# A hybrid block on one core: the expert bias as a constant feature, and sums of weighed values in the maxima's bank

## The chip, the cores and the metric

One core of a Trainium2 chip runs the kernel. The metric is the device time of one execution in microseconds. The kernel before was run three times.

## The reference

The block has four residual parts, over 4 sequences of 512 tokens with 128 features:

```python
x = x + attn_a(layernorm(x))   # 16 heads of 8, rope, causal softmax
x = x + ffn(layernorm(x))      # 8 experts, top 2 of a sigmoid gate, and one shared expert
x = x + attn_b(layernorm(x))   # short convolution, a scan over time, a gate
x = x + ffn(layernorm(x))      # the same weights again

# in ffn, H = 512, exact gelu:
h  = gelu(einsum('td,ehd->teh', xf, W1) + b1)
eo = einsum('teh,edh->ted', h, W2) + b2
combined = einsum('ted,te->td', eo, weights)
shared = gelu(xf @ Ws1.T + bs1) @ Ws2.T + bs2
```

`layernorm` has no scale and no shift, so the 128 features of a normed token sum to zero.

## The kernel before

**Attention** (about 26 to 225 us). The work goes by pairs of heads, 8 pairs for each sequence, 32 in all, numbered n. For pair n TensorE (PE) makes raw scores in three S units, of which VectorE (DVE) takes row maxima (`row_max`) and splits each into two bf16 numbers (`split_max`, L1883). PE turns them (`turn_max`, L1325), ScalarE (ACT) copies them out of PSUM (`copy_max`), and the SP queue places them by DMA as two more rows of the transposed queries (`place_max`, L623). Then PE makes transposed scores less the maximum in three T units (`scores_T`, L1340), ACT takes their exp (`exps`), and PE weighs the values with them (`weigh_values`). S runs two pairs ahead of T. After every second pair ACT copies the weighed values to SBUF (`take_weighed`, L960), PE turns and sums them with four fp32 products (`weighed_T`, L1375), and DVE divides by the sum of the exps (`divide`, L1891 and L1892).

PSUM has eight banks. Banks 0 to 5 are three slots of two, which the units of `ring_order` take in turn: S, T, the projections of the next sequence, the output projection, and the sums "w". A unit may start once the unit three places before it has been read. Bank 6 holds the weighed values, bank 7 (`Q2_BANK`) the turned maxima, each pair in one half of it.

Beside it the expert weights are loaded by ACT's queue (`ffn_loads`, L1020), and their largest magnitude is found on DVE in 16 pieces (`find_tops`). From pair 17 on ACT and DVE split the scaled weights into two f16 parts. GpSimd (POOL) does rope for the sequences 1 to 3 (`rope`, L768 and after), adds the output bias (`add_bias`), and reduces the bounds of the scales over partitions.

**Experts.** Each of the two ffn parts picks experts (`gates`, `choose`, `ranks`, `place`), and POOL scatters each token row, as two f16 parts scaled by `X_SCALE`, to its experts' lists in DRAM (L875). `map_tiles` (DVE) finds the expert of each of NT = 39 tiles of 128 rows. The tile stages (`tiles`, about 297 to 375 and 507 to 587 us) are a loop over k on PE: turn tile k (L1600), up products of tile k - 1, down products of tile k - 3 (L1626, L1627). Up is a bias product over 96 rows (L1606), then 12 products of 128 columns (L1612): high by high, low by high, high by low for each quarter of the 512 hidden features. ACT makes the gelu of tile k - 1 (L1155) and its high half (L1160), DVE the row's destination (L2123), the copy of the turned tile (L2129), the low half (L2135) and the sum of the down results (L2143). SP loads weights and rows, POOL scatters the results (L884). Tile s can have its gelu only once the low half of tile s - 3 is made, for three buffers.

The bias product multiplies `bias_rows` (each expert's bias in three bf16 parts, made on POOL by `bias_table`) by `which` (one column for each tile that picks the expert, made in `map_tiles`, L2098).

PE's order of work is written out by hand; each engine runs its own list in order, with waits on semaphores.

## Time and profile before

| | us |
|---|---|
| three runs | 608.64, 609.64, 613.06 |
| median | 609.64 |
| profiled execution | 606.08 |
| its span | 604.2 |

| engine | busy us | share of the span |
|---|---|---|
| PE, matmul | 501.5 | 83% |
| PE, weight load | 320.3 | 53% |
| DVE | 432.9 | 72% |
| ACT | 331.9 | 55% |
| POOL | 265.1 | 44% |

The mean granted clock of TensorE is 0.942 of full speed. A matmul's record is longer than the time until the next may start, since matmuls overlap: periods are read from starts. A wait is written with the engine and the line that ended it; where that engine had long been done, something else did. A releaser "remote" or "another core or an unknown queue" is one that the profile doesn't know.

### The profile page before, as it was taken

How to read it: one execution, taken by the hardware profiler on the slowest of the kernel's cores; microseconds unless marked ns; L12 is line 12 of the kernel's file. 1: busy time of each engine (PE TensorE's matmuls, PEld its weight loads, DVE VectorE, ACT ScalarE, POOL GpSimd, SP SyncE). 2: the span in 40 equal slices, each digit the busy share in tenths (PEclk: the TensorE clock that was granted, in tenths of full speed). 3: DMA queues.
4: the chain of work that ended last, by engine and by line, in shares of the span. 5: the costliest groups of instructions: out<-in, count | busy, mean ns of one | idle time of the engine just before them, and what ended most of it. 6: DMA issues, size and time to landing. Idle time of an engine off the chain costs nothing.

```text
span 604.2 us, 14288 instructions
## 1 busy us (share of the span) xinstructions
PE 501.5 (83%) x5019; PEld 320.3 (53%) x5021; DVE 432.9 (72%) x1162; ACT 331.9 (55%) x509; POOL 265.1 (44%) x247
## 2 busy tenths in 40 slices
PE   7778879878888888679999987879989977989950
PEld 2335556545656545334688775224545544878730
DVE  5658897686787968566377874798789663767745
ACT  1337556654777652546377863246657833757730
POOL 5509550045000037777046555373256770555550
PEclk9999999996999988888999999869999998999985
DMA  4863533441421370111588651997000016777516
GB/s 119 221 254 108 143 108 90 113 120 47 129 60 55 109 240 1 40 50 45 154 233 235 200 179 41 258 195 110 10 28 28 31 50 179 220 215 208 168 42 208
DMA packets 85708, 76.14 MB, mean 126 GB/s; under 512 B 9645, under 2 KB 72614, under 8 KB 85382
## 3 DMA queue, kind: packets, MB, share of 16 engines
q1 hardware_dynamic: 76320, 57.86, 36.6%
q0 software_dynamic: 4544, 9.38, 4.5%
q10 hardware_dynamic: 4774, 7.98, 3.7%
q8 instruction: 42, 0.69, 0.5%
q14 instruction: 28, 0.23, 0.1%
HBM read 37.88 MB, written 30.88 MB: 114 GB/s over the span
## 4 chain that ended last, share of the span: by engine, by line
PE 27%; DVE 9%; issue 5%; ACT 5%; another core or an unknown queue 4%; DMA 3%; POOL 1%; SPq 1%; ACTq 0%; DVEq 0%; POOLq 0%
PE ps L1612 6%; PE ps L1626 4%; PE ps L1627 3%; PE ps L1483 3%; DMA arena<-y_dram 2%; PE ps L1606 2%; DVE probs L2135 2%; ACT arena L1155 1%; PE ps L1560 1%; PE ps L1538 1%; DVE x_all L2164 1%; PE ps L1698 1%; DVE x_all L2160 1%; PE ps L1600 1%
## 5 line engine op out<-in xcount | busy, mean ns | idle before, releaser
L884 POOL DMA_INDIRECT y_dram<-arena,goes_to x78 | 85.0, 1090 | 90.5 <-DVE goes_to L2123 65.7
L1874 DVE TENSOR_REDUCE max_words<-ps 128x2 f32<-128x256 f32 (+3 forms) x128 | 98.0, 817 | 24.4 <-PE ps L1316 24.2
L955 ACT ACTIVATE probs<-ps 128x768 f32<-128x768 f32 (+1 forms) x96 | 81.1, 885 | 50.0 <-PE ps L1345 49.8
L730 POOL TENSOR_TENSOR rstd<-var_eps,minus_half 128x4 f32<-128x4 f32 x16 | 17.5, 1094 | 147.5 <-DVE var_eps L1841 147.5
L1155 ACT ACTIVATE arena<-ps,up_back 128x512 f32<-128x512 f32 x78 | 53.0, 680 | 52.1 <-PE ps L1612 28.6
L875 POOL DMA_INDIRECT rows_dram<-probs,idx x64 | 68.5, 1071 | 25.6 <-issue 18.6
L1626 PE MATMUL ps<-w,probs 128*128 x312 | 60.5, 273 | 11.7 <-DVE probs L2135 10.9
L1612 PE MATMUL ps<-arena 128*128 128x128 f16 x936 | 64.9, 219 | 4.0 <-DVE arena L2129 3.7
L2135 DVE SCALAR_TENSOR_TENSOR probs<-arena,hid_scale,probs 128x512 f16<-128x512 f32 x78 | 58.4, 748 | 11.5 <-ACT probs L1160 5.7
L1612 PEld LDWEIGHTS ps<-arena 128*128 128x128 f16 x936 | 57.8, 97 | 16.2 <-issue 8.7
L1483 PE MATMUL ps<-w,ident_f 128*128 128x512 f16 x184 | 56.3, 428 | 11.5 <-ACT arena L1111 3.3
L1160 ACT ACTIVATE probs<-arena,hid_scale 128x512 f16<-128x512 f32 x78 | 56.3, 722 | 2.6
L1627 PE MATMUL ps<-w,probs 128*128 x312 | 56.0, 219 | 0.6 <-issue 0.6
L2143 DVE TENSOR_REDUCE arena<-ps 128x128 f32<-128x256 f32 x78 | 32.9, 421 | 28.8 <-PE ps L1627 20.8
L1340 PE MATMUL ps<-heads_arena 64*128 64x512 bf16 (+3 forms) x256 | 38.2, 312 | 14.3 <-ACT probs L955 7.5
L1311 PE MATMUL ps<-heads_arena 62*128 62x128 bf16 (+3 forms) x256 | 36.5, 305 | 9.8 <-DVE max_words L1874 8.2
L1365 PE MATMUL ps<-probs,v_tok 128*32 128x256 f32 (+3 forms) x512 | 42.8, 452 | 2.0 <-ACT probs L955 2.0
L1626 PEld LDWEIGHTS ps<-w,probs 128*128 128x128 f16 x312 | 30.5, 98 | 18.6 <-issue 15.1
L1483 PEld LDWEIGHTS ps<-w,ident_f 128*128 128x128 f16 x184 | 18.0, 107 | 36.0 <-issue 13.7
L1316 PE MATMUL ps<-mask_qk,neg_eye 64*128 64x128 bf16 x512 | 34.3, 218 | 0.0
L1345 PE MATMUL ps<-mask_kq,neg_eye 64*128 64x128 bf16 x512 | 32.3, 221 | 0.0
L1627 PEld LDWEIGHTS ps<-w,probs 128*128 128x128 f16 x312 | 30.5, 98 | 1.1 <-issue 1.0
(242 smaller groups left out, 1033.7 us busy)
## 6 DMA issues: line engine op xcount, KB each, us to landing
arena<-weights_dram SPq DMA_DIRECT2D x78, 256.0 KB
rows_dram<-grids SPq DMA_DIRECT2D x64, 260.0 KB, 4.0
heads_arena<-q_words SPq DMA_DIRECT2D x45, 128.0 KB, 2.4
qk_sb<-rows_dram SPq DMA_DIRECT2D x78, 65.0 KB
arena<-in_w ACTq DMA_DIRECT2D x2, 2304.0 KB
weights_dram<-w SPq DMA_DIRECT2D x2, 1152.0 KB, 8.0
arena<-y_dram SPq DMA_DIRECT2D x16, 128.0 KB, 5.2
arena<-y_dram ACTq DMA_DIRECT2D x16, 128.0 KB, 5.3
```

Source lines behind the costliest of these rows:

```text
L875: nc.gpsimd.indirect_dma_start(rows_dram[r].ap(), bass.IndirectOffsetOnAxis(ap=idx[:, r, b, t, k:k + 1], axis=0), xrow_words_of(r, b)[:, t ...
L884: nc.gpsimd.indirect_dma_start(y_dram.ap(), bass.IndirectOffsetOnAxis(ap=goes_to[:, n % AT_GO:n % AT_GO + 1], axis=0), y_t[:, n % YT, :], ...
L955: nc.scalar.activation(probs[:, n % 2, :, PROB_AT[u]:PROB_AT[u] + size], ps[:, of:of + 2, 0:size], ACT.Exp).then_inc(slot_free[slot_of(("T ...
L1155: nc.scalar.activation(hid_t[:, n % HT, :], ps[:, of, :], ACT.Gelu, scale=up_back[:]).then_inc(bank_free[of], 1)
L1160: nc.scalar.activation(hid16_t[:, n % HT, 0, :], hid_t[:, n % HT, :], ACT.Identity, scale=hid_scale[:]).then_inc(high_t_ready, 1)
L1365: mm = pe.matmul(ps[group:group + OW, PV_BANK, j * P:L], v_flat[:, at_v:at_v + OW], probs[:, n % 2, h, at[j]:at[j] + L - P * j], start=(p ...
L1483: pe.matmul(ps[:, to, :], ident_f16[:], w1[:, 0, 0, :], start=True, stop=True, skip_group_check=True)
L1612: mm = pe.matmul(ps[:, to, c * P:(c + 1) * P], w1t[:, s % WT, w, c * P:(c + 1) * P], xgT[:, n % GT, v, :], start=False, stop=(v == 1), ski ...
L1626: pe.matmul(halves, hid16_t[:, n % HT, 0, c * P:(c + 1) * P], parts, start=(c == 0), stop=False, skip_group_check=True)
L1627: mm = pe.matmul(halves[:, 0, :], hid16_t[:, n % HT, 1, c * P:(c + 1) * P], parts[:, 0, :], start=False, stop=(c == C - 1), skip_group_che ...
L1874: ins = nc.vector.tensor_reduce(max_words[:, n % 2, :, t], ps[:, of:of + 2, o:o + keys], AX.X, ALU.max)
L2135: nc.vector.scalar_tensor_tensor(hid16_t[:, n % HT, 1, :], hid_t[:, n % HT, :], hid_scale[:], hid16_t[:, n % HT, 0, :], ALU.mult, ALU.subt ...
```

## The change

Two things are changed.

**The bias as a feature.** Since a normed token's features sum to zero, W1 x is also the sum over the first 127 features of (w_d - w_127) x_d. Feature 127 is then free: it carries the constant 1 (times `X_SCALE`, in the high part, and 0 in the low part), and row 127 of the experts' weights carries the bias. The host puts b1 into row 127 of `w1`, and gives `last_w1`, the row w_127 of all experts repeated for 128 partitions, 4096 fp32 values each. ACT's queue loads it into the room of the split weights, and POOL subtracts it from the raw weights after the first rope, in two instructions. `find_tops` takes the pieces of W2 first, and those of W1 after the subtraction. The bias product, its tables and their waits go, and the first up product of each quarter starts the accumulation. The shared expert keeps its bias in ACT's gelu.

**The sums in bank 7.** The maxima of all pairs now lie in the first quarter of the bank, and the sums of weighed values its upper half. The unit "w" leaves the ring. `weighed_T` stands before the third T unit, not after it, and waits for the copy of the next maximum and for the division before it; `turn_max` waits for the last division; ACT copies the weighed values before the first exp. The order in which banks are given after attention is changed too.

```diff
-        if n >= 2 and n % 2 == 0:
-            order += [("w", n // 2 - 1)]
-RINGS = {"all": (7, 1, 3, 5, 6, 2, 4, 0), "y": (0, 1), "wide": (2, 3, 4), "rest": (5, 6, 7)}
+RINGS = {"all": (1, 3, 5, 7, 6, 0, 2, 4), "y": (0, 1), "wide": (2, 3, 4), "rest": (5, 6, 7)}
...
+        def max_columns(n):
+            return ps[0:4 * TT, Q2_BANK, (n % 2) * (P // 2):(n % 2 + 1) * (P // 2)].bitcast(BF16)
+
+        def sums_at(start, end):
+            return ps[:, Q2_BANK, L // 2 + start:L // 2 + end]
...
@@ pool
             rope(1)
+            pool.wait_ge(ffn_in, 16 * len(ffn_loads))
+            pool.wait_ge(last_w1_loaded, 16)
+            for half in range(2):
+                of = slice(half * E * F // 2, (half + 1) * E * F // 2)
+                raw = arena[0:D - 1, of]
+                nc.gpsimd.tensor_tensor(raw, raw, last_w1[0:D - 1, of], ALU.subtract).then_inc(less_last, 1)
             add_bias(2)
             rope(2)
...
-            bias_table()
+            pool.wait_ge(pv_made, PAIRS)
+            set_constants(xrow)
@@ act
                 nc.scalar.dma_start(whole(dst), src).then_inc(ffn_in, 16)
+            nc.scalar.dma_start(last_w1, last_w1_in).then_inc(last_w1_loaded, 16)
...
-                exps(n, 0)
                 if n >= 2 and n % 2 == 0:
                     take_weighed(n // 2 - 1)
+                exps(n, 0)
                 exps(n, 1)
@@ pe, turn_max
                     pe.wait_ge(max_copied, n - 1)
+                if n >= 4:
+                    pe.wait_ge(sums_free, (n - 2) // 2)
@@ pe, weighed_T
-                to = give(("w", g))
+                if g >= 1:
+                    pe.wait_ge(sums_free, g)
+                pe.wait_ge(max_copied, min(2 * g + 4, PAIRS))
                 pe.wait_ge(weighed_ready, g + 1)
...
                 scores_T(n, 1)
-                scores_T(n, 2)
                 if n >= 2 and n % 2 == 0:
                     weighed_T(n // 2 - 1)
+                scores_T(n, 2)
@@ pe, tiles
-                pe.wait_ge(bias_ready, 1)
...
-                    pe.matmul(ps[:, to, :], bias_rows[0:BIAS_ROWS, :], which[0:BIAS_ROWS, s, :].unsqueeze(2).broadcast_to([BIAS_ROWS, C, P]),
-                              start=True, stop=False, skip_group_check=True)
...
@@ dve
+                if k == 0:
+                    dve.wait_ge(less_last, 1 if (piece + 1) * PIECE <= E * F // 2 else 2)
...
-                for c in range(C):
-                    nc.vector.tensor_scalar(which[:, :, c], expert_of[:], grids[:, MOD_AT + c:MOD_AT + c + 1], None, ALU.is_equal)
@@ host
-        "w1": w1.transpose(2, 0, 1),
+        "w1": np.concatenate([w1[:, :, 0:D - 1].transpose(2, 0, 1), np.concatenate([b1[0:E], w1[E:, :, D - 1]], 0)[None]], 0),
...
-        "b1e": np.tile(a["L0_ffn_b1"].reshape(E * C, P), (3, 1)),
+        "last_w1": np.repeat(w1[0:E, :, D - 1].reshape(1, E * F), P, 0),
```

## Rows read from the trace of the kernel before

**Rows 1.** Busy time by stretch: us, then each engine, clock, DMA share, GB/s.

```profile
core 0: us, PE busy (x) PEld busy (x) DVE busy (x) ACT busy (x) POOL busy (x), PEclk, DMA share, GB/s
40.00:80.00 40.00, 34.68 (x497) 21.45 (x499) 33.57 (x55) 25.07 (x40) 28.26 (x17) 1.00 0.38 109
302.00:374.00 72.00, 65.15 (x850) 54.98 (x847) 52.57 (x147) 49.88 (x74) 41.11 (x38) 1.00 0.63 185
510.00:585.00 75.00, 65.22 (x856) 55.34 (x853) 54.55 (x150) 51.87 (x76) 41.74 (x38) 1.00 0.61 182
```

**Rows 2.** Timeline of PE over one tile: start, length, work, idle before and releaser.

```profile
335.58 0.28 PE L1600 MATMUL ps<-ident_f,qk_sb 128*128 128x128 f16 x2
335.69 0.38 PE L1606 MATMUL ps<-weighed,bias_rows 96*128 96x512 bf16 x1
335.91 0.83 PE L1612 MATMUL ps<-arena 128*128 128x128 f16 x12
...
337.24 0.27 PE L1600 MATMUL ps<-ident_f,qk_sb 128*128 128x128 f16 x2
```

**Rows 3.** Timeline of PE and ACT, 329 to 334 us.

```profile
329.69 0.83 PE L1612 MATMUL ps<-arena 128*128 128x128 f16 x12
...
332.43 0.69 ACT L1155 ACTIVATE arena<-ps,up_back 128x512 f32<-128x512 f32 x1 [2.15 <-remote]
...
333.78 0.67 ACT L1155 ACTIVATE arena<-ps,up_back 128x512 f32<-128x512 f32 x1
```

**Rows 4.** Waits in the first tile stage, 300 to 375: total us, times, longest.

```profile
ACT arena L1155 <- remote: 8.4, 4, 2.2
...
PE ps L1626 <- DVE probs L2135: 5.6, 8, 1.5
```

**Rows 5.** Waits in the second tile stage, 510 to 585 us.

```profile
PE ps L1626 <- DVE probs L2135: 5.3, 8, 0.9
```

**Rows 6.** Timeline of DVE in the second map of tiles.

```profile
496.43 0.71 DVE L2098 TENSOR_SCALAR weighed<-weighed,grids 128x39 bf16<-128x39 f32 x4
```

**Rows 7.** Timelines of PE and of DVE in pair 22.

```profile
171.94 0.34 PE L1340 MATMUL ps<-heads_arena 64*128 64x384 bf16 x2
...
172.88 0.28 PE L1340 MATMUL ps<-heads_arena 64*128 64x256 bf16 x2 [0.49 <-ACT probs L955]
...
173.44 1.08 PE L1375 MATMUL ps<-fold,weighed 128*128 128x64 f32 x8
174.45 0.23 PE L1311 MATMUL ps<-heads_arena 62*128 62x128 bf16 x2
...
175.23 0.22 PE L1325 MATMUL ps<-ident,max_words 128*16 128x128 bf16 x1
...
173.49 0.17 DVE L1883 TENSOR_TENSOR max_words<-max_words 128x8 bf16<-128x8 f32 x1
174.55 0.26 DVE L1891 RECIPROCAL rec<-ps 128x16 f32<-128x16 f32 x1 [0.90 <-PE ps L1375]
174.84 0.29 DVE L1892 TENSOR_TENSOR att<-ps,rec 128x128 f32<-128x128 f32 x1
```

**Rows 8.** The start: SP's and PE's timelines, and the stretch of the loads.

```profile
30.81 13.97 SPq L623 DMA_DIRECT2D heads_arena<-max_rows  x6
...
40.27 0.39 PE L1340 MATMUL ps<-heads_arena 64*128 64x512 bf16 x2 [1.76 <-DMA heads_arena<-max_rows]
...
28.00:40.00 12.00, 8.64 (x63) 4.02 (x64) 7.16 (x11) 3.06 (x5) 2.04 (x2) 1.00 0.98 391
```

**Rows 9.** POOL's timeline at the second rope; all splits of maxima (min/median/max ns).

```profile
68.45 2.35 POOL L768 TENSOR_TENSOR rope_c<-q_words,k_words 128x1024 f32<-128x1024 f32 x1 [6.53 <-ACT q_words L991]
...
L1883 DVE TENSOR_TENSOR max_words<-max_words x32: 170/171/2040, 30.0 to 210.7; 128x8 bf16<-128x8 f32 x32
```

**Rows 10.** DVE and PE timelines at the bounds, and the stretch at half clock.

```profile
130.95 2.39 DVE L1932 SCALAR_TENSOR_TENSOR bounds<-bounds 128x1 f32<-128x1 f32 x1
...
136.97 0.61 PE L1311 MATMUL ps<-heads_arena 62*128 62x512 bf16 x2 [3.97 <-DVE max_words L1874]
...
135.10:145.30 10.20, 8.29 (x71) 5.26 (x73) 6.99 (x19) 1.81 (x3) 9.21 (x6) 0.50 0.06 16
```

More of the change, by code:

```diff
@@ L58 @@
 PIECE = X * F // PIECES
+TOPS_OF = [(k, piece) for k in (1, 0) for piece in range(PIECES)]
 PRODUCTS = [(0, 0), (1, 0), (0, 1)]
@@ L110, in ring_order @@
                 order += [(name, steps[n])]
-    return order + [("w", QUADS - 1), ("at", B - 1), ("wo", B - 1)]
+    return order + [("at", B - 1), ("wo", B - 1)]
 TURN = {unit: i for i, unit in enumerate(ring_order())}
@@ L383, in hybrid_block_kernel @@
         tile_row, weight_row, tile_expert = (weighed[:, NT * i:NT * (i + 1)].bitcast(I32) for i in range(4, 7))
-        which = part(weighed, 7 * NT, [NT, C], BF16)
         expert_of, tiles_past, first_row, list_end = (weighed[:, NT * i:NT * (i + 1)] for i in range(4))
@@ L831, in residual, with set_constants @@
                 nc.gpsimd.tensor_tensor(x_all[:, b], x_all[:, b], xsf[:, b], ALU.add).then_inc(residual_ready, 1)
[L833 to L849 removed]
+            def set_constants(rows):
+                nc.gpsimd.memset(rows[:, :, :, D - 1], X_SCALE)
+                link(nc.gpsimd.memset(rows[:, :, :, 2 * D - 1], 0.0))
             def split_rows(r, b):
@@ L858, in split_rows @@
                     pool.wait_ge(scattered[b - 2], 16 * 2 * TT * 2)
-                high, low = (xrow_of(r, b)[:, :, k * D:(k + 1) * D] for k in range(2))
-                link(nc.gpsimd.tensor_copy(high, xf_of(r, b)))
-                nc.gpsimd.tensor_tensor(low, xf_of(r, b), high, ALU.subtract).then_inc(rows_ready, 1)
+                if g == 0:
+                    set_constants(xrow4)
+                high, low = (xrow_of(r, b)[:, :, k * D:(k + 1) * D - 1] for k in range(2))
+                tokens = xf_of(r, b)[:, :, 0:D - 1]
+                link(nc.gpsimd.tensor_copy(high, tokens))
+                nc.gpsimd.tensor_tensor(low, tokens, high, ALU.subtract).then_inc(rows_ready, 1)
             def scatter(r, b):
@@ L977, in copy_max @@
                     act.wait_ge(max_placed[n % 2], 32 * (n // 2))
-                nc.scalar.copy(max_rows[:, n % 2, :], half_bank(n)[0:4 * TT, 0:P]).then_inc(max_copied, 1)
+                nc.scalar.copy(max_rows[:, n % 2, :], max_columns(n)).then_inc(max_copied, 1)
             def pre_queries(a):
@@ L1094, in last_rows_high @@
                 act.wait_ge(scattered[B - 3], 16 * 2 * TT * 2)
-                nc.scalar.copy(xrow_of(1, B - 1)[:, :, 0:D], xf_of(1, B - 1)).then_inc(last_high_ready, 1)
+                nc.scalar.copy(xrow_of(1, B - 1)[:, :, 0:D - 1], xf_of(1, B - 1)[:, :, 0:D - 1]).then_inc(last_high_ready, 1)
             def gates(r, b):
@@ L1886, in divide @@
                 a, q = divmod(g, 4)
-                of = take(("w", g))
+                dve.wait_ge(sums_full, g + 1)
                 if q == 0 and a >= 1:
                     dve.wait_ge(slot_full[slot_of(("at", a - 1))], filled(("at", a - 1)))
-                sums = ps[:, of, 0:TT * Q * VW].rearrange("p (t h w) -> p t h w", t=TT, h=Q)
+                sums = sums_at(0, TT * Q * VW).rearrange("p (t h w) -> p t h w", t=TT, h=Q)
                 core_link(nc.vector.reciprocal(rec[:], sums[:, :, :, HD]))
@@ L2050, in last_rows_low @@
                 dve.wait_ge(last_high_ready, 1)
-                high, low = (xrow_of(1, B - 1)[:, :, v * D:(v + 1) * D] for v in range(2))
-                nc.vector.tensor_tensor(low, xf_of(1, B - 1), high, ALU.subtract).then_inc(last_rows_ready, 1)
+                high, low = (xrow_of(1, B - 1)[:, :, v * D:(v + 1) * D - 1] for v in range(2))
+                nc.vector.tensor_tensor(low, xf_of(1, B - 1)[:, :, 0:D - 1], high, ALU.subtract).then_inc(last_rows_ready, 1)
             def place(r, b):
@@ L2332, in shape_constants @@
     grids[:, ONES_AT:ONES_AT + E] = 1.0
-    for c in range(C):
-        grids[:, MOD_AT + c] = np.where((rows < BIAS_ROWS) & (rows % C == c), rows // C % E, -1)
-    grids[:, PART_AT:PART_AT + 3] = rows[:, None] // (E * C) == np.arange(3)[None, :]
     grids[:, TOK_AT:TOK_AT + B * TT] = SPARE + 2 * (rows[:, None] + P * np.arange(B * TT))
```

62 lines of the change are left out of this document (20 added, 42 removed).

## Prediction, before the change was run

> **What bounds the kernel now.** I read the stretches first. In the two tile stages PE is busy 65 of 72 and 65 of 75 us at full clock, with ACT and DVE near 50 each [rows 1]: PE is the first suspect, with little room behind it. In attention (the row of 40 to 80 us stands for it) PE is busy 34.7 and DVE 33.6 of 40: no engine is full, two are nearly, so there the order of the units in the three-slot ring decides.
>
> Next the timeline of one tile. From the turn of one tile to that of the next, 335.58 to 337.24, PE needs 1.66 us without a gap, and the bias product stands 0.11 us behind the turn in the same queue. Its record says 0.38 us, but the first up product starts 0.22 us after it (512 columns at 2.4 GHz are 0.213): the 0.38 holds overlap, and 0.22 is what PE spends [rows 2].
>
> Then what else a tile needs. ACT's two passes repeat every 333.78 - 332.43 = 1.35 us when work is queued [rows 3]. That is below 1.66, and it stays below 1.44 = 1.66 - 0.22, by 0.09 only. And ACT is not always fed: the up products of one tile started at 329.69 and were through at 330.52, yet ACT's gelu, idle 2.15 us, began at 332.43, its releaser unknown to the profile [rows 3]. PE's results are thus sometimes seen some 2 us late, for a reason that I can't name. PE pays when its down product waits for the halves that DVE makes of that late gelu: 8 such waits, 5.6 us, in the first tile stage, 8 waits, 5.3 us, in the second [rows 4, 5].
>
> **Part 1: no bias product.** One for each of 39 tiles in two stages, 78 products go, 78 x 0.22 = 17.2 us of PE. Not all comes back. Between the up products of a tile and its down product lie two periods of PE's loop, so the slack that hides the chain gelu, high, low shrinks by 2 x 0.22 = 0.44 us. Each of the 8 waits of a stage grows by that: 8 x 0.44 = 3.5. A stage of 39 tiles gives 39 x 0.22 - 3.5 = 5.1 us, two give **10.2 us**. Ends: 17.2 if no wait grows; 4 if ACT, with only 0.09 us per tile to catch up, never recovers from one late signal before the next. I take the middle since only 8 of 39 tiles show the wait.
>
> POOL's table of ten small steps and the wait on it go too. Nothing in the waits names it as a releaser: 0. Of the map of tiles, four instructions on DVE go, 0.71 us in one row with overlap, 0.6 in its place [rows 6]. In the second stage PE and SP wait for the map: **-0.6 us**; in the first it lies beside shared products: 0. DVE, ACT and POOL now split 127 of 128 columns, and POOL sets a few constants, beside the gates and the shared products: 0.
>
> **Part 2: sums in the maxima's bank.** Take an even pair [rows 7]. PE's second T unit starts at 171.94 and takes 0.34. The third waits for ACT to free its slot and starts at 172.88. The sums, 173.44 to 174.45, come next, 1.0 us with nothing beside them on PE, and only then the next pair's first scores. DVE, done with the maxima at 173.66, sits idle 0.90 us until it can divide at 174.55. After the change ACT copies the weighed values ahead of its first exp (the values are weighed before the pair's T units start), and the sums run from about 172.3 to 173.3, over the 0.6 us gap. The third unit slips 0.4 us, the next scores start 0.55 to 0.8 earlier, and the division directly follows the maxima. ACT's last exp then ends about as before, which holds the gain at the lower value: 15 even pairs x 0.55 = **8.2 us**. The sixteenth sums lie behind the loop: 0. Ends: 15 x 1.0 = 15 (the whole sums hidden) and 0.
>
> The change adds two waits. The sums wait for the copy of the maximum of the pair ahead; ACT does that first in the iteration: 0. The turn of the maximum waits for the division; behind it on PE stand the weighing of values and the T units. Before, the turn came at 175.23, and the division that it must now await ended at 174.84 + 0.29 = 175.13, in time. Afterwards PE arrives at about 174.4, and the division ends at 173.66 + 0.55 = 174.2: 0.2 us to spare. I cost it at 0; where DVE is late the turn loses up to the 0.55.
>
> **Part 3: the new weight copies.** ACT issues one more load of 128 x 4096 x 4 bytes = 2.1 MB. At the 391 GB/s of the loads' stretch it takes 5.4 us [rows 8]. It queues behind the others, so it ends at about 45 instead of 40 us. The first maxima's placement was issued at 30.81, and the first T unit could start only at 40.27, with the placement as its releaser [rows 8]. Placements of the first two pairs should slip through in the small tables ahead of the new load: **+0.5 us**, at worst 5.4. The one issue on ACT lies in a wait for PE: 0.
>
> POOL subtracts the last row in two instructions of 2048 elements a partition. Its 1024-element ones take 2.35 us, so 4.7 each, 9.4 together, right after the first rope. POOL stood idle 6.53 us there, until 68.45; the rest delays the second rope by about 3 us; that happens in pair 6, and its placements are due in pairs 10 to 13: 0 [rows 9]. But while POOL computes, DVE's small step that splits a maximum, 171 ns at the median, has taken up to 2040 [rows 9]. One or two splits fall into the 9.4 us. DVE mostly has slack there, since PE is busy with projections: **+1.0 us**, ends 0 and 9.4.
>
> The Trainium skill (SBUF — State Buffer, Who interferes with whom) calls the port pair of these two engines an exclusive lock for a whole instruction, taken by a DVE instruction with two SBUF inputs. The trace agrees (2040 ns against 171). By it one split may wait 4.7 us here, where the longest in the trace lost 1.9.
>
> Finding the weights' maxima only changes order; DVE reaches the subtracted pieces in pair 8: 0. The new bank order moves no unit ahead of another: 0.
>
> **Sum.** -10.2 - 0.6 - 8.2 + 0.5 + 1.0 = -17.5 us. The profiled execution took 606.1 (its span is 604.2, and 1.9 lie around it): 588.6. The median of the runs, 609.6, is 3.6 above it, so for the median I say **592 us**.
>
> **Rivals.**
> - Forecast, 586 to 597: 0.48.
> - Both ends good, -17.2 and about -12: 582 to 585. For it: the 0.09 us left to ACT is positive. Against: the late signals. 0.12.
> - The turn's wait replaces the ring's: it takes 0.55 on each even pair, the 8.2 are gone, 600. For: only 0.2 us to spare. Against: DVE divides 0.9 us earlier. 0.13.
> - Late signals eat the tile gain: ACT (1.35 a tile) plus its unfed time becomes the bound, the 10.2 are gone, 602. 0.09.
> - The port lock (the second of the two pages): splits stand behind both POOL instructions in full, 9.4 instead of 1.0, 600. 0.07.
> - The load delays the first T unit by its whole length: 5.4 instead of 0.5, 597. 0.04.
> - It doesn't do what it says: both the order and the product were hidden, 606 to 610. The gapless 1.66 us speaks against it. 0.03.
> - Slower: DVE held up by POOL starves PE, and the clock falls. At 130.95 a step on one column took 2.39 us beside POOL's rope, PE then sat idle 3.97 us, and from 135.1 the granted clock was 0.50 (1.2 GHz) for 10.2 us [rows 10]. I price that event at 4 us idle and half of PE's 8.3 busy ones at the low clock, 8 us in all. To end above 615.7 it takes (615.7 - 592)/8 = 3 new ones; the subtraction spans at most two splits. 0.04.
>
> **How the numbers follow.** A measurement of this kernel can't tell less than about 1% (6.1 us) from no change. Below 603.5 lie the forecast, the good end, most of the turn, port and load rivals, and part of the late-signal one: 0.86. Within 1%: 0.10. Slower: 0.04. For 8 in 10 the range runs from 583 (most of the good end) to 602 (the single lost gains).
>
> **What would show it.** In the profile after: a turn-to-turn period of 1.44 us where PE has no gap; waits of the down product for DVE's halves at least as many as before, and longer by some 0.4 each; sums ahead of the third T unit, and DVE's wait ahead of its reciprocal gone (0.90 each before); no wait of the turn for a division; a split of over 2 us between 60 and 70 us; the first T unit at 40 to 41 us. I am wrong if the tile period stays near 1.66, if the even pairs are not shorter, or if the clock falls at new places.

## The result, and the profile after

The changed kernel took 601.6 us (median of 4 runs, 599.7 to 604.2), the kernel before 611.3 us beside it (4 runs). The ratio is 0.987, 95% interval 0.984 to 0.991: 1.3% faster, where 2.9% was forecast. Some executions run in a second, slower state at a lower mean clock: ratios below leave them out, median times don't, and the profiles of a2 and b2 are of such executions. The profiled execution took 599.7 us with a span of 597.5, against 606.1 and 604.2 before: 6.7 us less, where 17.5 were forecast. Milestones of the two spans, each the start of a record, show where they came from (in us; "first turn" and "last reduction" are the first and last step of a tile stage on TensorE and on VectorE):

| stretch | before | after | change | forecast |
|---|---|---|---|---|
| start to first T unit | 40.3 | 40.5 | +0.3 | +0.5 |
| first T unit of pair 0 to that of pair 31 | 177.9 | 174.7 | -3.2 | -7.2 |
| first tile stage (first turn to last reduction) | 75.8 | 75.1 | -0.7 | -5.1 |
| between the stages (last reduction to first turn) | 133.7 | 131.2 | -2.4 | -0.6 |
| second tile stage | 77.5 | 77.1 | -0.3 | -5.1 |

The tile stages gave 1.0 of 10.2 us, the attention 3.2 of 7.2. Busy time by stretch, to be read against [rows 1]:

```profile
core 0: us, PE busy (x) PEld busy (x) DVE busy (x) ACT busy (x) POOL busy (x), PEclk, DMA share, GB/s
40.00:80.00 40.00, 34.45 (x499) 21.75 (x499) 33.67 (x56) 25.19 (x40) 34.64 (x18) 1.00 0.52 157
299.00:369.00 70.00, 59.19 (x811) 52.84 (x809) 51.63 (x146) 50.03 (x74) 40.43 (x37) 0.98 0.65 193
506.00:578.00 72.00, 58.55 (x799) 51.84 (x796) 51.47 (x146) 49.63 (x73) 39.44 (x38) 0.98 0.63 187
```

In the tile stages PE was busy 65 of 72 us and is now busy 59 of 70. The product is off PE, and the time went into idling. The clock column falls from 1.00 to 0.98: in this trace each stage of the changed kernel holds 3.4 us at half clock (1.2 GHz), from 316.2 and from 534.7 us, and before has no such stretch in its stages:

```profile
316.20:319.60 3.40, 3.40 (x28) 3.00 (x27) 2.37 (x7) 2.11 (x4) 1.43 (x2) 0.50 0.85 253
534.70:538.10 3.40, 2.78 (x24) 2.33 (x22) 2.98 (x9) 2.37 (x4) 1.18 (x2) 0.50 0.85 271
```

Ahead of both PE stood several times for 0.4 to 0.7 us: for DVE's copy, for the halves, or for nothing that the profile names. At full clock its work there would take half as long, so an estimate of the loss is up to 1.7 and 1.4 us. The prediction had named clock falls at new places as a sign of being wrong. PE's and ACT's timelines over one tile, which answer [rows 2, 3]:

```profile
326.44 0.28 PE L1598 MATMUL ps<-ident_f,qk_sb 128*128 128x128 f16 x2
326.56 0.83 PE L1608 MATMUL ps<-arena 128*128 128x128 f16 x12
...
327.88 0.28 PE L1598 MATMUL ps<-ident_f,qk_sb 128*128 128x128 f16 x2
...
329.44 0.69 ACT L1149 ACTIVATE arena<-ps,up_back 128x512 f32<-128x512 f32 x1 [2.10 <-remote]
...
330.42 0.78 PE L1608 MATMUL ps<-arena 128*128 128x128 f16 x11 [0.62 <-DVE arena L2125]
```

From turn to turn it is 1.44 us, as forecast. But the up products that were through at 327.4 reach ACT at 329.4, as late as in [rows 3], and then PE stands for DVE's copy. The recorded times of the semaphores say what is late. The increments of this up product and of three later products of PE (ends by the records 327.39, 328.05, 328.16, 328.83) are recorded at 329.41, 329.50, 329.55 and 329.70, nearly together, while PE's records run on. So I call these late signals of PE, not late products. Waits of the first tile stage, for [rows 4]:

```profile
ACT arena L1149 <- remote: 10.5, 5, 2.3
PEld ps L1622 <- issue: 7.6, 11, 1.1
...
PEld ps L1608 <- issue: 6.1, 7, 1.8
...
PE ps L1608 <- DVE arena L2125: 5.0, 7, 1.6
PE ps L1622 <- DVE probs L2131: 3.4, 5, 0.9
```

PE's waits have spread over more places than the one that I had priced, and at that one (the last line) they are fewer and shorter in sum than before (5 and 3.4 us, before 8 and 5.6). The second stage's answer to [rows 5], the waits for the halves, 7 and 5.2 us where before had 8 and 5.3:

```profile
PE ps L1622 <- DVE probs L2131: 5.2, 7, 1.1
```

The first T unit, for [rows 8]:

```profile
40.53 0.39 PE L1336 MATMUL ps<-heads_arena 64*128 64x512 bf16 x2 [1.60 <-DMA heads_arena<-max_rows]
```

The attention. PE and DVE in pair 22, for [rows 7]:

```profile
171.95 0.34 PE L1336 MATMUL ps<-heads_arena 64*128 64x384 bf16 x2
...
172.33 1.10 PE L1373 MATMUL ps<-fold,weighed 128*128 128x64 f32 x8
173.37 0.28 PE L1336 MATMUL ps<-heads_arena 64*128 64x256 bf16 x2
...
174.53 0.22 PE L1321 MATMUL ps<-ident,max_words 128*16 128x128 bf16 x1
...
173.51 0.17 DVE L1879 TENSOR_TENSOR max_words<-max_words 128x8 bf16<-128x8 f32 x1
173.59 0.25 DVE L1887 RECIPROCAL rec<-ps 128x16 f32<-128x16 f32 x1
173.88 0.29 DVE L1888 TENSOR_TENSOR att<-ps,rec 128x128 f32<-128x128 f32 x1
```

The sums stand ahead of the third T unit, DVE divides right behind its split, and the turn (174.53) comes 0.36 us after the division's end (174.17). All as forecast, with 0.36 us to spare instead of 0.2.

And the clock. PE stood 2.76 us for DVE, whose little statistic was slow beside POOL's rope, itself put off by the subtraction, and then ran 6.8 us at half clock (1.2 GHz). No such stretch lies there in the trace of before. Timelines of POOL (the two subtractions in one row), DVE and PE, and the stretch itself:

```profile
60.89 9.04 POOL L797 TENSOR_TENSOR arena<-arena,w 127x2048 f32<-127x2048 f32 x2
...
83.45 1.40 DVE L1832 TENSOR_TENSOR mean_sum<-stats 128x4 f32<-128x4 f32 x1
...
87.77 0.61 PE L1305 MATMUL ps<-heads_arena 62*128 62x512 bf16 x2 [2.76 <-DVE max_words L1870]
```

```profile
87.50:94.30 6.80, 6.49 (x59) 4.55 (x63) 5.08 (x10) 1.87 (x3) 0.00 (x0) 0.50 0.09 19
```

### The profile page after: what moved, and what is told of

The parts are those of the page before. It is cut to its first block, busy times and chain, and to the rows that moved or that the text cites. A ratio compares the mean times of both kernels' runs of the same rounds, so it can differ in the third digit from the quotient of the medians.

```text
span 597.5 us, 14116 instructions
## 1 busy us (share of the span) xinstructions
PE 488.9 (82%) x4941; PEld 319.0 (53%) x4943; DVE 431.1 (72%) x1154; ACT 332.1 (56%) x509; POOL 265.0 (44%) x242
## 3 DMA queue, kind: packets, MB, share of 16 engines
q0 software_dynamic: 4544, 9.38, 4.6%
## 4 chain that ended last, share of the span: by engine, by line
PE 45%; DVE 24%; ACT 9%; another core or an unknown queue 7%; issue 6%; DMA 5%; POOL 2%; SPq 2%; DVEq 0%; ACTq 0%; POOLq 0%
PE ps L1608 6%; DVE max_words L1870 5%; PE ps L1622 4%; PE ps L1361 4%; PE ps L1482 3%; PE ps L1336 3%; PE ps L1373 3%; PE ps L1285 2%; PE ps L1623 2%; ACT arena L1149 2%; ACT probs L948 2%; PE ps L1305 2%; PE ps L1559 2%; DMA arena<-y_dram 2%
## 5 line engine op out<-in xcount | busy, mean ns | idle before, releaser
L876 POOL DMA_INDIRECT y_dram<-arena,goes_to x78 | 83.5, 1071 | 91.8 <-DVE goes_to L2119 69.8
L727 POOL TENSOR_TENSOR rstd<-var_eps,minus_half 128x4 f32<-128x4 f32 x16 | 17.5, 1091 | 144.4 <-DVE var_eps L1837 144.4
L1149 ACT ACTIVATE arena<-ps,up_back 128x512 f32<-128x512 f32 x78 | 53.0, 679 | 48.7 <-PE ps L1608 23.3
L867 POOL DMA_INDIRECT rows_dram<-probs,idx x64 | 66.0, 1031 | 27.6 <-issue 18.0
L1608 PE MATMUL ps<-arena 128*128 128x128 f16 x936 | 65.9, 221 | 11.4 <-DVE arena L2125 11.4
L1622 PE MATMUL ps<-w,probs 128*128 x312 | 62.3, 278 | 14.3 <-DVE probs L2131 10.4
L1608 PEld LDWEIGHTS ps<-arena 128*128 128x128 f16 x936 | 56.1, 99 | 14.0 <-issue 13.7
L1482 PE MATMUL ps<-w,ident_f 128*128 128x512 f16 x184 | 53.1, 406 | 10.0 <-ACT arena L1105 3.4
L1623 PE MATMUL ps<-w,probs 128*128 x312 | 57.5, 222 | 0.9 <-issue 0.9
```

The source lines that it names most:

```text
L867: nc.gpsimd.indirect_dma_start(rows_dram[r].ap(), bass.IndirectOffsetOnAxis(ap=idx[:, r, b, t, k:k + 1], axis=0), xrow_words_of(r, b)[:, t ...
L876: nc.gpsimd.indirect_dma_start(y_dram.ap(), bass.IndirectOffsetOnAxis(ap=goes_to[:, n % AT_GO:n % AT_GO + 1], axis=0), y_t[:, n % YT, :], ...
L1149: nc.scalar.activation(hid_t[:, n % HT, :], ps[:, of, :], ACT.Gelu, scale=up_back[:]).then_inc(bank_free[of], 1)
L1482: pe.matmul(ps[:, to, :], ident_f16[:], w1[:, 0, 0, :], start=True, stop=True, skip_group_check=True)
L1608: mm = pe.matmul(ps[:, to, c * P:(c + 1) * P], w1t[:, s % WT, w, c * P:(c + 1) * P], xgT[:, n % GT, v, :], start=((w, v) == (0, 0)), stop= ...
L1622: pe.matmul(halves, hid16_t[:, n % HT, 0, c * P:(c + 1) * P], parts, start=(c == 0), stop=False, skip_group_check=True)
```

## The experiments

Eighteen runs were made, on four chips (a, b and d on one each, c and e on the fourth); b1 and c3 are the changed kernel again, and b2 and c4 are the same kernel. One table for all; "stages" are their lengths in the profile, "late" counts the tiles of each stage (of 39) whose first activation on ScalarE began over 0.7 us after the up product's end, with ScalarE idle just before it. Besides what is said of each below, a4, b2, b3, c4 and e2 hold a3's edit too, and b3 has b2's groups of register loads. Before took 583.2 us beside the first four, 610.6 beside b1 to b4, 604.0 beside c1 to c4, 608.0 beside the d runs and 608.6 beside the e runs.

| run | us | ratio to before (95%) | stages | late |
|---|---|---|---|---|
| before, first measurement | 611.3 | 1 | 75.8, 77.5 | 11, 7 |
| after, first measurement | 601.6 | 0.987 (0.984-0.991) | 75.1, 77.1 | 8, 10 |
| a1_bias_only | 577.7 | 0.991 (0.987-0.995) | 63.7, 65.3 | 0, 0 |
| a2_sums_only | 577.5 | 0.983 (0.974-0.991) | 67.7, 67.9 | 0, 0 |
| a3_sub_later | 571.0 | 0.980 (0.972-0.989) | 63.8, 65.8 | 0, 0 |
| a4_deep | 573.0 | 0.976 (0.966-0.987) | 63.5, 66.1 | 0, 0 |
| b1_after | 598.7 | 0.984 (0.978-0.989) | 75.3, 77.5 | 8, 9 |
| b2_spread | 603.5 | 0.987 (0.981-0.992) | 74.7, 79.1 | 11, 8 |
| b3_deep_spread | 602.5 | 0.981 (0.974-0.988) | 72.6, 74.9 | 9, 8 |
| b4_deep_before | 603.7 | 0.990 (0.983-0.996) | 72.5, 73.2 | 10, 10 |
| c1_less_act_dve | 595.5 | 0.987 (0.978-0.996) | 73.5, 75.1 | 13, 13 |
| c2_less_pe | 595.1 | 0.986 (0.982-0.991) | 72.7, 74.0 | 12, 12 |
| c3_after | 597.6 | 0.990 (0.986-0.993) | 74.0, 77.1 | 9, 10 |
| c4_spread | 597.7 | 0.990 (0.982-0.997) | 73.7, 77.5 | 8, 9 |
| d1_plain | 578.5 | 0.952 (0.944-0.960) | 65.0, 66.1 | 0, 0 |
| d2_few_weights | 597.8 | 0.984 (0.976-0.992) | 74.4, 75.4 | 9, 9 |
| d3_static | 565.8 | 0.931 (0.923-0.940) | 59.2, 59.2 | 0, 0 |
| e1_before_plain | 589.0 | 0.973 (0.964-0.981) | 67.6, 67.7 | 0, 0 |
| e2_one_load | 604.6 | 0.992 (0.987-0.997) | 74.5, 76.0 | 7, 11 |
| e3_plain_one_load | 570.3 | 0.940 (0.932-0.947) | 60.4, 61.2 | 0, 0 |

**Each part alone.** a1 is before with parts 1 and 3, a2 before with part 2, both whole sets of edits of the diff. a3 is the changed kernel with this edit:

```
             add_bias(2)
             rope(2)
             far_root(3)
+            (the two subtractions and their waits, taken from ahead of add_bias(2))
```

> The kernel before with the bias as feature 127 alone (no bias product, last weight row taken off by GpSimd), its ring, its order of units and its row sums as before. Theory: the two tile stages got shorter by only 0.7 and 0.3 us in the changed kernel's profile, the stretch between them by 2.4 us, and GpSimd's 9 us subtraction pushed the second image's rope behind a norm statistic, after which TensorE stood and ran at half clock for 6.8 us (3.5 us lost). Then this kernel ends at 606 to 611 us, that is 0 to 5 us below before. Rival: the removed product does save 0.2 us in each tile and the sums' move ate it; then this kernel is at 595 to 600 us.

> The kernel before with the other part alone: sums of weighed values in the maxima's bank, between the second and the third transposed unit, the weighed copy ahead of the first exponential; the bias product stays. Theory: even pairs are 0.35 us and odd pairs 0.3 to 0.6 us shorter (4.87 and 4.6 to 4.8 us in the changed kernel where they ran at full clock, 5.21 and 5.0 to 5.25 before), so 5 to 8 us come off and no half-clock stretch arises at 87 us: 603 to 606 us. Rival: the attention gain of the changed kernel was only the 3.2 us that its profile shows, and this kernel is at 607 to 609 us.

> The changed kernel with GpSimd's subtraction of the last weight row (2 instructions of 4.5 us) moved behind the second image's rope and the third far root. Theory: the rope ends 9 us earlier, the norm statistic of pair 7 isn't slowed beside it (0.17 instead of 1.40 us), TensorE does not stand at 85 us and the half-clock stretch at 87 to 94 us is gone: 3.5 us less than the changed kernel, 597.5 to 598.5 us. Rival: clock stretches come at some place anyway, or the subtraction now delays the first weight pieces on VectorE and they delay the maxima; then 600 to 603 us.

The chip, or its state, decided more than the kernels: before itself took 583 us, and in these four traces not one signal was late. Against before, a1 came out 5.5 us lower and a2 1.7% faster, each at or a little beyond the better end of what I expected. Here the bias product's removal does shorten the stages, 67.7 and 67.9 us (a2) to 63.8 and 65.8 (a3). Of the clock, my theory fell: a2 has no subtraction and drops to half clock at 87.4 us all the same. The attention's sizes: 181.2 us in a1, 174.8 in a2, and a3, whose trace has no such stretch there, 173.6.

**More distance between the engines.**

```
-XG, GT, HT, YT, AT_GO = 7, 3, 3, 8, 16
+XG, GT, HT, YT, AT_GO = 7, 4, 4, 8, 16
+AHEAD = 2        # up(k - 2) behind turn(k); down(s) behind up(s + 3)
```

> The kernel with the subtraction moved, and in both tile stages more distance between the engines: a tile is turned two steps ahead of its up product (one before), four buffers for turned tiles and for hidden tiles (three before), the down product three up products behind (two before). The arithmetic per tile is the same. Theory (the loop TensorE, VectorE's copy, TensorE and the loop TensorE, ScalarE, VectorE, TensorE are too short to cover signals of TensorE that come 2 to 3 us late, so that a tile takes 1.9 us although the products of one take 1.44): the tile stages fall from 75 and 77 us to 60 to 68 us each, and the whole to 575 to 588 us. Rival 1: the late signals are real stalls of TensorE, which no distance covers; then the stages stay within 2 us of what they were, and the whole is within 3 us of the kernel with the moved subtraction. Rival 2: something else with a rate of 1.9 us per tile bounds them (the loads of rows and weights, the stores of results); same time as rival 1, but then TensorE waits for loads.

> The changed kernel itself, again. In its first profile TensorE's signals to ScalarE and VectorE came 2 to 3 us late in bursts in both tile stages (ScalarE's first activation began 0.5 us after the up product's end in the median, over 0.7 us 8 and 10 times in a stage), and so they did in the profile of before (0.32 us, 11 and 7 times). In the four kernels run on another chip they came late not once (0.04 us in the median), and there the tile stages took 63.7 and 65.3 us without the bias product, 67.7 and 67.9 us with it, instead of 75 to 77 us. Theory: the late signals belong to the chip or its state, not to the kernel; where they are absent the median tile period is 1.44 us and this kernel is 2.0 to 2.7% faster than before, where they are there 1.0 to 1.6%. Rival: the changed kernel as it is (subtraction early) calls them forth; then the stages are above 70 us also beside a before near 583 us.

> As the last, with more distance between the engines: turned two steps ahead of the up product, four buffers, the down product three up products behind. Theory of late signals: on a chip where they come, the stages fall from about 75 us to 62 to 68 us, and this kernel is 3 to 5% faster than the changed one; on a chip where they don't come (median 0.04 us), it gains nothing over the kernel without the distance, as in the earlier run (63.5 and 66.1 beside 63.8 and 65.8 us). Rival: late signals are real stalls of TensorE and no distance covers them; no gain on either.

> The kernel before with the same distance between the engines, bias product kept. Theory: on a chip without late signals its period is TensorE's 1.66 us already and nothing changes (ratio 0.995 to 1.005); on one with them the stages of 75.8 and 77.5 us fall to 66 to 70 us, and the whole by 2 to 3%. Rival as above: no change on either.

a4 gained nothing where no signal is late (63.5 and 66.1). On the next chip the late signals were back, in the changed kernel as it is too (b1, at 0.984 where 1.0 to 1.6% was expected). There the distance covers a part of them, 2.5 to 4.3 us a stage (b3 against b1, b4 against the first trace of before), short of the 6 to 13 expected. In the times b4 shows it (0.990, 0.983 to 0.996); b3 beside b1 doesn't (0.981 and 0.984, with wide intervals).

**SyncE's register loads.** a3's stages have holes that a2's don't. PE's timeline at one, then the transfers on SyncE's queue before it:

```profile
521.74 0.28 PE L1598 MATMUL ps<-ident_f,qk_sb 128*128 128x128 f16 x2
523.91 0.49 PE L1608 MATMUL ps<-arena 128*128 128x128 f16 x6 [1.89 <-issue]
...
516.67 0.33 SPq L676 DMA_DIRECT2D arena<-weights_dram  x1
517.28 0.33 SPq L684 DMA_DIRECT2D qk_sb<-rows_dram  x1
520.95 0.34 SPq L676 DMA_DIRECT2D arena<-weights_dram  x1
```

Between 517.6 and 520.9 SyncE issues nothing: it stands in a register load of 2.81 us from 517.65 on.

```
+WEIGHT_GROUPS = (0, 8, 20, 33, NT)   # b2, c4: for weights_from, instead of GROUPS
```

> The changed kernel with the subtraction moved behind the rope, and with SyncE's register loads of the weight rows taken at tiles 8, 20 and 33 instead of 4, 13 and 26, so that none follows one of the tile rows (4, 13, 26) within a few tiles. In the kernel with the subtraction alone moved, SyncE stood in two loads of 2.97 and 2.81 us at 512.95 and 517.65, its next weights were issued at 520.95, and TensorE, now at 1.44 us a tile, stood 1.89 us at 522 for them; two more such holes (1.62 and 1.33 us) are in its stages, none with the bias product left in. Theory: SyncE's queue is the next bound where TensorE is faster; the holes go, the stages fall by 1 to 3 us each: 1 to 5 us below the kernel with the subtraction alone moved (63.8 and 65.8 us become 61 to 64). Rival: the holes are of the weights' transfers themselves (a landing takes 2.9 us there) or of TensorE's own instruction fetches; then nothing changes, within 1 us.

> The changed kernel with the subtraction behind the rope and SyncE's register loads of weight rows at tiles 8, 20 and 33, as in the earlier run, which fell on a chip with late signals (stages of 74.7 and 79.1 us in its profile). Theory: on a chip without late signals the holes of 1.3 to 1.9 us for weights go and the stages are 1 to 3 us shorter than 63.8 and 65.8 us; on one with them there is no difference from the changed kernel beyond the 1% that its measurement scatters. Rival: the holes have another cause, no change on either.

Both fell on chips with late signals and show no difference there: 0.990 for c4 and for c3, the changed kernel beside it, 0.987 and 0.984 for b2 and b1. The question was taken up again below.

**Who is full?** c1 takes `0:F // 2` of the columns for the high part on ScalarE and the low part on VectorE, and the down product reads them twice; c2 takes `PRODUCTS[0::2]` in the up product, and so leaves out the low part of the weights.

> The changed kernel with less work on ScalarE and VectorE in the tiles: the high part and the low part of the hidden values are taken of 256 of the 512 columns, and the down product reads these twice, so the result is not the reference's; TensorE's work per tile is the same. Theory of thin margins: ScalarE needs 0.69 + 0.72 = 1.41 us a tile, VectorE is busy 1.40 us of it, TensorE 1.44. At 1.66 us a tile ScalarE makes up for a late signal at 0.25 us a tile, at 1.44 us it hardly can, so that with late signals a stage takes ScalarE's 55 us plus the 16 to 19 us that it stood for them, with or without the bias product. With 1.1 to 1.2 us a tile it catches up again: on a chip with late signals the stages of 75 and 77 us fall to 65 to 70, the whole is 3 to 5% faster than before; on one without them the stages stay at 63 to 66 us, TensorE's 1.44 us a tile. Rival: the late signals are stalls of TensorE, which no faster follower makes good: the stages stay within 2 us of 75 and 77.

> The changed kernel with less work on TensorE in the tiles: the up product leaves out the low part of the weights (4 of 12 matmuls of 128 columns, 0.22 us a tile), so the result is not the reference's to full accuracy. Theory of thin margins: ScalarE's 1.41 us a tile is the bound then, so the stages stay within 2 us of the changed kernel's, on a chip with late signals (75 and 77 us) and on one without (64 to 66 us, at most 1 to 2 us less for a period of 1.41 instead of 1.44). Rival, TensorE is the bound and its late signals are its stalls: 39 times 0.22 us = 8 us less in each stage.

> The changed kernel itself, beside the others. Where before is near 583 us and the median gap from the end of the up product to ScalarE is 0.04 us, the stages are 63 to 66 us and the kernel is 2.0 to 2.7% faster than before; where before is near 611 us, the stages are 75 and 77 us and it is 1.3 to 1.7% faster, as twice before. If both kinds of chip give the same ratio, the tile stages aren't what the gain depends on.

Thin margins are not it. In c1 ScalarE's two passes take 1.19 us a tile instead of 1.40, and VectorE is busy 1.11 us a tile instead of 1.41; beside c3 the stages lose 0.4 and 2.0 us, where I expected 5 to 12. In c2 TensorE has 0.22 us a tile less to do, and they lose 1.3 and 3.1, of 8: the second is more than the theory allowed, and both are far from the rival. No engine is full. c1 over 63 us of its first stage: ScalarE is busy 39.8 of them, and VectorE 37.8.

```profile
297.00:360.00 63.00, 52.21 (x753) 47.85 (x751) 37.76 (x136) 39.78 (x68) 34.80 (x34) 1.00 0.68 205
```

**What makes the signals late?** In d1 the stores of the tiles' results are plain:

```
-nc.gpsimd.indirect_dma_start(y_dram.ap(), bass.IndirectOffsetOnAxis(ap=goes_to[...], axis=0), y_t[:, n % YT, :], None)
+nc.gpsimd.dma_start(y_dram.ap()[at:at + P, :], y_t[:, n % YT, :])
```

d2 returns from `load_weights(s)` for `s >= WT`. TensorE's wait for the weights is fitted to that. d3 is d1 with fixed slices in place of every `bass.ds(...)` in the stages, and without SyncE's register loads.

> The changed kernel with the tiles' result rows stored by a plain transfer to fixed rows (same bytes, same queue of GpSimd) in place of the indirect one, so the results land in the wrong rows. What delays TensorE's signals is open: on three of four chips so far they come 1 to 3 us late in the tile stages (ScalarE stands 14 to 19 us a stage for them, beyond 0.3 us each), on one they never do, and ever without effect of less work on any engine (stages of 73.5 and 75.1 us with less on ScalarE and VectorE, 72.7 and 74.0 with less on TensorE, 74.0 and 77.1 us as changed). They come where GpSimd issues indirect transfers (scatter of rows at 225 to 285 and 380 to 495 us, the tile stages) and never in the attention. Theory 1, the indirect transfers do it: no late signals here, stages of 62 to 66 us. Theory 2, the traffic of the loads does it: as changed, 74 to 77 us.

> The changed kernel with the weights of a tile loaded for the first 8 tiles of a stage only and used again by the later ones, so the results are of wrong experts' weights: 256 of some 385 KB a tile are not moved. Theory 2 (the loads' traffic, 75 to 90% of the transfer engines' time in these stages, keeps TensorE's signals back): no late signals or half as many, stages of 60 to 68 us. Theory 1 (indirect transfers): stages as changed, 74 to 77 us. On a chip without late signals both give 61 to 65 us and the run says only what the loads cost there.

> The kernel with plain stores and, besides, with rows, weights and the expert of the down product taken from fixed places, so that SyncE and TensorE compute no address from a register and SyncE loads none; wrong rows and weights, the traffic is the same. Theory 3 (register loads of 2.5 to 3 us on SyncE and TensorE's address registers hold TensorE's queue up): no late signals here while the run with plain stores alone has them, stages of 62 to 66 us. Theories 1 and 2: same as the run with plain stores alone.

Theory 1 stands, and theories 2 and 3 fall. Without two thirds of the bytes of a tile (d2) nothing changes: the transfer engines' share falls to 0.28, where c3 has 0.65, and the stages stay at 74.4 and 75.4.

```profile
300.00:368.00 68.00, 57.25 (x795) 51.58 (x792) 50.79 (x145) 49.95 (x73) 39.13 (x36) 0.98 0.28 76
```

With plain stores not one signal is late, and the stages fall by some 10 us each. The stores in the first trace of the changed kernel (the page's costliest groups: busy us, mean ns, idle before, releaser), and ScalarE's first activation:

```profile
L876 POOL DMA_INDIRECT y_dram<-arena,goes_to x78 | 83.5, 1071 | 91.8 <-DVE goes_to L2119 69.8
...
L1149 ACT ACTIVATE arena<-ps,up_back 128x512 f32<-128x512 f32 x78 | 53.0, 679 | 48.7 <-PE ps L1608 23.3
```

and in d1:

```profile
L877 POOL DMA_DIRECT2D y_dram<-arena x78 | 42.1, 540 | 112.6 <-DVE goes_to L2119 88.9
...
L1149 ACT ACTIVATE arena<-ps,up_back 128x512 f32<-128x512 f32 x78 | 53.5, 686 | 26.6 <-PE ps L1608 26.5
```

ScalarE's idle time ahead of it fell from 48.7 to 26.6 us, and what is left ends with TensorE's up product. d1's stores go over the same software queue with as many packets (4544, 9.38 MB on both pages). So it is the indirect form, the scattered rows that it writes, or the 1071 instead of 540 ns that it takes on GpSimd, not the queue nor the bytes; these weren't told apart. The Trainium skill (DMA: Bandwidth & Descriptors, Latency and other measured facts) guesses at contention of GpSimd's descriptor rings at SBUF's ports, as the reason why DMA engines 7 and 15 are slower than the others. It says nothing there of TensorE's signals, and its guess speaks of all of GpSimd's software transfers, where the plain ones did no harm here. No run shows the mechanism.

**Before with plain stores, and one register load in place of two.**

```
+weights_at.extend(((row >> 11) << 7).with_bounds(min_val=0, max_val=E * P) for row in at)
```

> The kernel before, bias product kept, with the tiles' results stored by a plain transfer to fixed rows in place of the indirect one (results in wrong rows), as it was done with the changed kernel: there the late signals vanished and the stages fell from some 75 and 77 us to 65.0 and 66.1 on a chip where before takes 608 us. Theory (indirect transfers delay TensorE's signals on most chips, and that hid the bias product's 0.22 us a tile): here the signals are on time as well, the tile period is 1.66 us, the stages are 67 to 69 us, so that without late signals the change takes 2 to 4 us off each, and this kernel is 2.3 to 3.2% faster than before (the changed one with plain stores was 4.8% faster). Rival: the stores' faster issue (0.54 instead of 1.1 us on GpSimd) is what helped, and before, whose tiles are slower, gains less than half of it: stages above 71 us.

> The changed kernel, its arithmetic whole, with the subtraction behind the rope and with one register load for a group of tiles on SyncE in place of two: the row of a tile's weights is worked out from its row in the lists (the list's number times 128) in SyncE's registers. SyncE issues 2 transfers a tile in 1.09 us and stood 15 us a stage in register loads (0.98 to 2.97 us each), 57 us of work beside TensorE's 56. Theory: on a chip without late signals the stages fall from 63.8 and 65.8 us to 59.5 to 62, the whole is 3.5 to 4.5% faster than before; on one with late signals they still set the pace (1.8 us a tile), 73 to 77 us, and it is 1 to 2% faster. Rival: computed addresses cost SyncE more per transfer than the loads that go; no change on either.

> The changed kernel with plain stores (results in wrong rows) and with one register load for a group in place of two. With everything at fixed places the stages took 59.2 us each, with plain stores alone 65.0 and 66.1. Theory: SyncE's queue is what is left of the gap to 1.44 us a tile; half of its register loads gone, the stages take 60 to 62.5 us on any chip. Rival: TensorE's or SyncE's computed addresses make the gap; the stages stay at 64 to 66 us.

e1 has before's 1.66 us a tile, without late signals: 67.6 and 67.7 us, as a2 had. The rival for it, stages above 71 us, falls. So the change is worth 2.6 and 1.6 us a stage in d1, and 7.2 and 6.5 in e3, with half of SyncE's loads gone. A stretch inside the first stage of e1:

```profile
305.00:362.00 57.00, 56.96 (x789) 51.12 (x788) 51.50 (x137) 48.17 (x69) 18.28 (x34) 1.00 0.75 229
```

of d1:

```profile
297.00:350.00 53.00, 49.75 (x727) 47.34 (x726) 46.81 (x133) 46.34 (x67) 17.30 (x32) 0.97 0.80 249
```

of e3:

```profile
299.00:349.00 50.00, 49.44 (x753) 47.59 (x751) 48.30 (x138) 47.94 (x69) 18.38 (x34) 1.00 0.82 254
```

and of d3:

```profile
300.00:348.00 48.00, 48.00 (x736) 46.51 (x734) 47.12 (x135) 46.90 (x68) 17.84 (x33) 1.00 0.84 252
```

With the bias product PE is busy all the time. Without it PE stands 3.3 of 53 us, 0.6 of 50 with one load, and not at all with none. d1's stretch includes 3.4 us at half clock (from 334.6 us), which are part of its difference from e3; d1's second stage (66.1) has none and e3's is still 4.9 us shorter. e2, with indirect stores and a3's edit, met late signals (7 and 11) on the same chip as e3, took 74.5 and 76.0 us where e3 takes 60.4 and 61.2, and is no faster than the changed kernel: 0.992. Where late signals come, they set the pace.

## Why the prediction was right or wrong

**The tile period: right, 1.44 us.** The median period is 1.44 us in a1, a3, a4, d1, d3 and e3, 1.66 in a2 and e1.

**Bias product, -10.2 us: the failed step.** It came to -1.0 in the first measurement. The step that failed is the price of the late signals in that term, "each of the 8 waits of a stage grows by" 0.44 us, 3.5 us a stage; the stages lost 8.1 of the 8.6 us of the product on average. I saw the late signals [rows 3], priced them by the 8 waits of the down product alone [rows 4, 5], and let each grow by that. The runs show three faults. The late signals are no offset of eight tiles; they hold the stage to 1.8 to 1.9 us a tile on average (from a stage's first up product to its last) whatever the engines have to do (c1 1.79 and 1.81, the changed kernel 1.83 and 1.87, before 1.84 and 1.89), and only more distance brings it a little lower (b4 1.71). Their cost on the changed kernel moved to waits that before hardly had: PE's up product waits for DVE's copy 11.4 us in all, 3.7 before. And my end of 4 us, "if ACT never recovers", was no end, since it left ACT's capacity as the worst bound; c1 shows that the capacity doesn't matter. The rival "late signals eat the tile gain", 602 us at 0.09, gave the measured time to within 0.4 us. It should have had much of the forecast's 0.48: a wait of 2 us with a releaser that the profile can't name is a bound of unknown kind, not a surcharge. So its number is luck in part: its mechanism (ACT plus unfed time) was wrong as well, by c1. (The end "582 to 585" of another rival is misadded: with its two terms the sum gives 581.) New clock falls in the stages, which I had priced only beside GpSimd's work in attention, take their part too: of 16 traces without the bias product 8 have a half-clock stretch that begins over 5 us before a stage's end and inside it, of 4 traces with it none.

**Where no signal is late** the term was still too large: -4.2 us over both stages (d1 against e1, 131.1 and 135.2) and -5.9 (a3 against a2), with -13.7 reached in e3. What took the rest was neither ACT nor DVE but SyncE. It issues two transfers a tile in 1.09 us and stands in four register loads a stage of 1 to 3 us, some 10 us together. By these numbers it can catch up 0.57 us a tile at 1.66, but only 0.35 at 1.44. The prediction left SyncE's queue in a stage out, though it had priced the queues at the start.

**Sums in the maxima's bank, -8.2, and subtraction, +1.0: right in sum where both clocks fall, 2 us too large where neither does.** Where the clock is full, even pairs shrank less than forecast, mostly from 5.21 to 4.88 us, and odd ones, which I held at nothing, by up to 0.65 (pair 23, 5.25 to 4.60). The length of the attention (from the first T unit of pair 0 to that of pair 31) goes with a half-clock stretch that begins near 88 us in most traces. With it, before's attention took 181.6 and 181.8 us (b4, e1), and the changed one with the subtraction ahead of the rope, in nine traces where the stretch begins at 85 to 91 us, 173.8 to 175.3, mean 174.6: -7.1, with -7.2 forecast. Without it before's took 177.9 in one trace, and the changed one with the subtraction behind the rope 171.7 to 173.6 in five, mean 172.9: some -5. The subtraction's +1.0 isn't seen: a2, without it, took 174.8, and a1, with before's order and the subtraction, 181.2. The -3.2 of the first pair of traces set an execution of before that had escaped that stretch against one of after that had not.

**The clock.** What I read from those two traces, that the subtraction causes the fall, isn't so: e1 and b4 fall at 88.9 to 89.9 us without any subtraction, behind the 1.5 us that PE always stands for DVE there. Of six traces with the subtraction behind the rope five (a3, a4, b2, b3, c4) lack it, but e2 has it, at 88.1 us, and took 174.7 us of attention as the changed kernel does. In the times of c4 against c3 nothing is seen of it. Why the fall comes in most executions and not in all stays open.

**The port.** The subtraction cost a split 0.82 us at 64.64 instead of 0.17, and the longest split, beside the rope behind it, is 2.36. The rule of the Trainium skill (SBUF — State Buffer, Who interferes with whom), the pair locked for the whole instruction, is borne out to 0.03 us: the statistic above ended at 83.45 + 1.40 = 84.85, POOL's rope instruction at 84.83. In a3 the split ended at 90.34, with POOL's first subtraction over at 90.3:

```profile
85.81 9.00 POOL L800 TENSOR_TENSOR arena<-arena,w 127x2048 f32<-127x2048 f32 x2
...
88.78 1.56 DVE L1879 TENSOR_TENSOR max_words<-max_words 128x8 bf16<-128x8 f32 x1
```

The step waits for what is left of the instruction, so a price of 4.7 each was a worst case that didn't occur.

**Extra load, +0.5: right** (+0.3, first T unit at 40.5). **Map, -0.6: can't be told.** The stretch between the stages took 131.2, 128.4 and 129.6 us in three executions of the changed kernel.

**The turn's wait: right**, 0.36 us to spare in pair 22, and one such wait in the whole attention, of 0.2 us.

No version was shown to beat the changed kernel with its results whole. d1, d3, e1 and e3 store results in wrong rows, c1, c2 and d2 leave out part of the arithmetic or of the weights. A way to store the tiles in order and gather them afterwards would move the indirect transfers out of the stage; it wasn't tried.

## What to carry to other kernels

An idle engine whose releaser the profile can't name, while the producer's records end 2 us earlier, is a bound to be found before any work is taken off an engine: look what the otherwise idle queues do in that stretch. Here an indirect store a tile held three tuned engines to 1.8 us a tile. When a loop gets faster, add up the queue that feeds it too, register loads included (here 1.09 us of issues a tile and some 10 us of loads in a stage, against 1.44 us a tile). Compare a stretch of two traces only where both have the same stretches at half clock. And measure on more than one chip: one of the six measurements here met no late signal.

## What the hardware showed that I had not expected

- In the tile stages TensorE's signals come up to 3 us late where GpSimd issues an indirect store for each tile (1.07 us each), in all 12 traces of five sessions on at least three chips, and in none of 4 on another chip, where the same kernel before is 3 to 5% faster (583 us against 604 to 611). With plain stores, 4 traces on two of the affected chips, none is late.
- They don't depend on the loads' traffic: with the transfer engines' share at 0.28 instead of 0.65 there were 9 and 9 late tiles, as with it.
- A register load on SyncE for 9 to 13 tiles took 1.0 to 3.1 us, and in that time its queue issued nothing.
- Without the bias product TensorE's clock falls inside the tile stages in 8 of 16 traces, for some 3.4 us at a time; with it in none of 4.
